# Cross-attention in fp32 on one core: three score banks, values of two tiles per block, row sums in a maximum buffer

## The reference

```
xn     = layernorm(x) * gamma + beta            # x [2, 512, 1024]
Q      = split_heads(xn @ Wq.T)                 # 32 heads of 32
K = V  = split_heads(ctx)                       # ctx [2, 1024, 1024]
scores = einsum('bhsd,bhtd->bhst', Q, K) / sqrt(32)
scores = where(mask, scores, -inf)
attn   = softmax(scores, -1) @ V
out    = x + attn.reshape(2, 512, 1024) @ Wout.T
```

## Time and profile before

| | us |
|---|---|
| three runs | 741.23 median, 739.92 to 744.85 |
| the profiled execution | 742.85 |
| its span, first to last instruction | 741.0 |

### The profile page before, as it was taken

How to read it: one execution, slowest core, us unless ns; L and a number is a source line. 1 busy time by engine, 2 the same in 40 slices (tenths; PEclk the granted TensorE clock), 3 DMA queues, 4 the chain that set the end, 5 groups by cost and what they waited for, 6 DMA issues and landing times.

```text
span 741.0 us, 10854 instructions
## 1 busy us (share of the span) xinstructions
PE 692.4 (93%) x3585; PEld 397.8 (54%) x3585; DVE 484.0 (65%) x496; ACT 350.1 (47%) x613; POOL 391.7 (53%) x106
## 2 busy tenths in 40 slices
PE   2789999878999999999999999999999999699998
PEld 2578788533444454444444444444444444378886
DVE  6762442057687878878788788887888677723231
ACT  3741112334565666656666566665665666300000
POOL 1000000047396797877978779688796798800000
PEclk9999999879999999999999999999999999999999
DMA  9620100515516235253351532515425104031331
GB/s 345 169 71 29 58 0 1 128 39 128 124 42 151 64 96 129 59 128 72 85 142 43 128 82 77 152 33 127 101 58 128 57 1 144 29 113 64 107 113 57
DMA packets 39518, 68.10 MB, mean 92 GB/s; under 512 B 5284, under 2 KB 21798, under 8 KB 39470
## 3 DMA queue, kind: packets, MB, share of 16 engines
q1 hardware_dynamic: 39444, 67.64, 33.2%
q10 hardware_dynamic: 36, 0.01, 0.0%
HBM read 25.18 MB, written 4.19 MB: 40 GB/s over the span
## 4 chain that ended last, share of the span: by engine, by line
PE 84%; DVE 6%; SPq 3%; DMA 2%; ACT 2%; issue 1%; POOL 1%; ACTq 0%; POOLq 0%; DVEq 0%
PE SX L903 18%; PE MX L883 17%; PE PV L919 16%; PE MX L1047 12%; PE SM L909 6%; PE PV L846 5%; PE SM L846 4%; DVE mx L703 2%; PE MX L823 2%; POOL acc L470 1%; PE MX L895 1%; PE SX L838 1%; DMA PR<-in_x 1%; PE MX L889 1%; ACT PR L504 1%
## 5 line engine op out<-in xcount | busy, mean ns | idle before, releaser
L703 DVE TENSOR_REDUCE mx<-MX 128x1 f32<-128x1024 f32 x256 | 303.1, 1220 | 139.6 <-PE MX L883 139.3
L587 ACT ACTIVATE PR<-SX 128x512 f32<-128x512 f32 x512 | 277.4, 594 | 187.4 <-PE SX L903 187.3
L470 POOL TENSOR_TENSOR acc<-acc,PR 128x2048 f32<-128x2048 f32 x64 | 293.5, 4586 | 31.9 <-ACT PR L587 25.4
L470 POOL TENSOR_TENSOR acc<-PR 128x2048 f32<-128x2048 f32 x16 | 73.3, 4580 | 222.0 <-ACT PR L587 143.5
L903 PE MATMUL SX<-R 99*128 99x512 f32 x512 | 180.1, 431 | 2.3 <-ACT PR L587 1.5
L883 PE MATMUL MX<-R 97*128 97x512 f32 x512 | 164.0, 417 | 17.0 <-DVE mx L703 7.2
L903 PEld LDWEIGHTS SX<-R 99*128 99x128 f32 x512 | 88.4, 189 | 112.2 <-ACT PR L587 91.8
L883 PEld LDWEIGHTS MX<-R 97*128 97x128 f32 x512 | 89.2, 189 | 105.1 <-DVE mx L703 63.3
L919 PE MATMUL PV<-PR,C 128*32 128x512 f32 x1024 | 138.7, 614 | 0.1
L1047 PE MATMUL MX<-R 128*128 128x512 f32 x192 | 46.8, 404 | 5.6 <-DVE R L782 5.6
L791 DVE TENSOR_TENSOR PR<-PR,MX 128x512 f32<-128x512 f32 x16 | 11.0, 688 | 58.5 <-PE MX L1047 56.9
(11 more groups left out here) (75 smaller groups left out, 517.7 us busy)
## 6 DMA issues: line engine op xcount, KB each, us to landing
R<-KTh SPq DMA_DIRECT2D x64, 256.0 KB, 4.3
PR<-in_x SPq DMA_DIRECT2D x16, 512.0 KB, 4.2
C<-in_ctx SPq DMA_DIRECT2D x16, 512.0 KB, 3.5
R<-KTl SPq DMA_DIRECT2D x64, 128.0 KB, 3.8
R<-QT SPq DMA_DIRECT2D x64, 128.0 KB, 2.5
acc<-in_L_xattn_Wq SPq DMA_DIRECT2D x8, 512.0 KB, 3.6
R<-QT SPq DMA_DIRECT2D x64, 64.0 KB, 2.1
C<-in_L_xattn_Wout SPq DMA_DIRECT2D x8, 512.0 KB, 3.2
```

The source lines that it names most:

```text
L470: nc.gpsimd.tensor_tensor(acc[:, :, :], a, PR[:, tt % RING, :, :], ALU.add).then_inc(pool_used, 1)
L587: nc.scalar.activation(PR[:, tt % RING, h, :], SX[h % 2][:, :], ACT.Exp, scale=SCALE).then_inc(exp_done, 1)
L703: nc.vector.tensor_reduce(mx[:, u % 2, c:c + 1], MX[par][:, :], mybir.AxisListType.X, ALU.max, negate=True).then_inc(mx_freed, 1)
```

## The change

- **Banks.** SM is gone; SX has three banks, used in turn. A score waits for the exp of the score three before it.
- **Slots.** A step is four slots of two tiles instead of eight tiles. A slot on TensorE: scores of heads 0, 1, 2 of the first tile; items; head 3; items; heads 0 and 1 of the second tile; items; heads 2 and 3; items; then values of the tiles `2k-1` and `2k` in one block.
- **Sums.** GpSimd adds tiles 0 to 5; tiles 6 and 7 and `acc` are multiplied by ones in one block, as an item `sums` in an MX buffer, at the end of slot 0 of the next step, right behind values of tile 7. `invert_sums` part 0 reads that buffer and frees it; parts 1 and 2 are in slot 1. So a step has 19 items, not 18. In the last step sums go to SX[0].
- **Bias.** The maxima lie as 16 columns in the order of the items, one transpose instead of four, and high and low parts are 16 x 128, not 4 x 512.
- **Queries.** `split_queries` stands after the first `max` of slot 0, not before `key_low`. SP issues the key rows before it waits for the split queries, and both before the load of values.
- **Items.** STEP and FIRST_STEP are new tables.

```diff
-POOL_TILES = (0, 1, 2, 4, 5, 6)
+BANKS = 3
+PROBS = TT * HPG
+POOL_TILES = (0, 1, 2, 3, 4, 5)
+DIRECT_TILES = (6, 7)
+GROUPED = [((0, 0), (0, 1), (0, 2)), ((0, 3),), ((1, 0), (1, 1)), ((1, 2), (1, 3))]
-SUMS_AT = (2, 5, 7)
+SUMS_AT = ((1, 0), (1, 1))
 FIRST_STEP = [
-    ([], []),
-    ([], maxima(1, 0, 1)),
...
+    ([], maxima(1, 0), maxima(1, 1), maxima(1, 2)),
...
 STEP = [
-    ([], keys(2)),
-    (maxima(1, 4), maxima(1, 5, 6)),
-    ([], maxima(1, 7, 8)),
-    ([], maxima(1, 9, 10)),
-    (maxima(1, 11), maxima(1, 12, 13)),
-    ([], maxima(1, 14, 15)),
-    ([], maxima(2, 0) + bias(1)),
-    (maxima(2, 1), maxima(2, 2, 3)),
+    (keys(2), maxima(1, 5), maxima(1, 6), maxima(1, 7) + sums(-1)),
+    (maxima(1, 8), maxima(1, 9), maxima(1, 10), maxima(1, 11)),
+    (maxima(1, 12), maxima(1, 13), maxima(1, 14), maxima(1, 15)),
+    (bias(1) + maxima(2, 0), maxima(2, 1), maxima(2, 2), maxima(2, 3, 4)),
 ]
...
             def bias_item(n, u, par):
-                for st in range(ST):
-                    ins = nc.tensor.transpose(MX[par][:, st * P:(st + 1) * P], mx[:, u % 2, st * HPG:st * HPG + P], ident[:, :])
-                ins.then_inc(bt_ready, 1)
+                nc.tensor.transpose(MX[par][:, 0:P], mx[:, u % 2, :], ident[:, :]).then_inc(bt_ready, 1)
...
+            def row_sums(n, bank):
+
+                for tt in DIRECT_TILES:
+                    sum_probs(bank, lambda h: PR[:, tt % RING, h, :], tt == DIRECT_TILES[0], False).then_inc(tile_used, 1)
                 pe.wait_ge(pool_used, ADDS * n + 2 * ADDS)
-                sum_probs(lambda h: acc[:, h, :], False, True).then_inc(sums_done, 1)
+                sum_probs(bank, lambda h: acc[:, h, :], False, True).then_inc(sums_done, 1)
...
+                for k, slot in enumerate(items):
+                    for j, (group, part) in enumerate(zip(GROUPED, slot)):
+                        for b, h in group:
+                            score(n, u, 2 * k + b, h)
+                        if j == len(slot) - 1 and k == 0 and not first:
+                            for item in part[:-1]:
+                                mx_item(*item)
+                            values(n - 1, u + RING - 1, TT - 1)
+                            mx_item(*part[-1])
                         else:
+                            for item in part:
+                                mx_item(*item)
+                    if k > 0:
+                        values(n, u, 2 * k - 1)
+                    values(n, u, 2 * k)
...
                 for k, slot in enumerate(items):
                     for j, part in enumerate(slot):
...
+                            if kind == "sums":
+                                invert_sums(n + a, 0, MX[at % 2][:, 0:S])
+                                dve.wait_ge(sums_turned, n + a + 1)
+                                dve.sem_inc(mx_freed, 1)
+                            at += 1
+                        if (k, j) == (1 if first else 0, 1) and n + 2 < STEPS:
+                            split_queries(n + 2)
```

More of the change, by code:

```diff
@@ L602, in high_and_bias, with step @@
                 return at
[L604 to L607, removed]
+            def step(n, items, at, first=False):
+                for k, slot in enumerate(items):
+                    for group, part in zip(GROUPED, slot):
+                        for b, h in group:
+                            exp(n, 2 * k + b, h)
+                        at = high_and_bias(n, part, at)
+                    if k == 0 and not first:
                         pv_copy(n - 1)
[L609 to L613, removed]
+            step(0, FIRST_STEP, FIRST_PARITY, first=True)
             with act.Fori(0, LOOPS) as j:
                 for u in range(1, RING + 1):
[L616 to L618 removed]
+                    step(RING * j + u, STEP, step_parity(u))
+            for n in APART[:-1]:
+                step(n, items_of(n), step_parity(n))
+            step(STEPS - 1, items_of(STEPS - 1), LAST_PARITY)
             pv_copy(STEPS - 1)
@@ L749, in wout_parts, with step @@
                                         ALU.subtract).then_inc(mx_freed, 1)
[L751 to L766, removed]
+            def step(n, u, items, at, first=False):
+                for k, slot in enumerate(items):
+                    for j, part in enumerate(slot):
+                        for kind, a, i in part:
+                            if kind == "keys":
+                                key_low(n + a, at % 2)
+                            if kind == "bias":
+                                bias_low(n + a, at % 2)
+                            if kind == "wout":
+                                wout_parts(i, at % 2)
+                            if kind == "max":
+                                maximum(n + a, u + a, i, at % 2)
+                            if kind == "sums":
[5 more added lines that the diff above has]
+                            split_queries(n + 2)
+                        if (k, j) in SUMS_AT and not first:
+                            invert_sums(n - 1, 1 + SUMS_AT.index((k, j)))
             step(0, 0, FIRST_STEP, FIRST_PARITY, first=True)
@@ new lines, in mx_item @@
+                def mx_item(kind, a, i):
+                    nonlocal at, freed, last_kind
+                    pe.wait_ge(mx_freed, freed - (kind != "bias" or last_kind != ("max", M_ITEMS - 1)))
+                    if kind == "keys":
+                        keys_item(n + a, u + a, at % 2, loads)
+                    elif kind == "bias":
+                        bias_item(n + a, u + a, at % 2)
+                    elif kind == "wout":
+                        wout_item(i, at % 2)
+                    elif kind == "sums":
+                        row_sums(n + a, MX[at % 2][:, 0:S])
+                    else:
+                        if first and i == 0:
+                            pe.wait_ge(rows_in[a], LATER_ROWS)
+                        max_item(n + a, u + a, i, at % 2)
+                    at += 1
+                    freed = freed + 1
+                    last_kind = (kind, i)
```

170 lines of the change are left out of this document (60 added, 110 removed).

## The result

The changed kernel takes **799.73 us** (median of 4 runs, 798.91 to 800.74), the kernel before on the same chip 743.04 (739.92 to 745.46): 1.0761 times as long, 95% interval 1.0732 to 1.0789. The forecast was 788, its range 764 to 812. The profiled execution took 800.44 us and its span is 798.6, 57.6 more than the span before.

What follows compares the result with a forecast made beforehand. TensorE was taken to bound the kernel, busy 692.4 of 741.0 us. Terms 38 (steps) + 4.5 (step 0) + 1.8 (end) + 2 (clock) = 46.3 on the profiled 742.85 gave 789, or 788 on the median's scale; range 764 to 812.

Steps and rivals of the forecast that it cites:

- The step: Steps 1 to 13: 33.5 us each with waits for MX, 2.9 more than before, 38 us in all; chance 0.62.
- The wait for keys: Slot 0: TensorE waits 1.6 us before maximum 6, until the buffer of keys comes back.
- the one before sums: End of slot 0: TensorE waits 0.7 us before sums, until maximum 6 frees its buffer.
- Slot 3: Last slot of a step: a wait of 1.25 us behind bias, then five maxima; 8.9 us instead of 6.3.
- The split: Query split on VectorE in slot 0: 1.1 us for both parts, with GpSimd idle, instead of 3.1.
- Rival 2: Slot 0: a GpSimd add catches the split, wait 2.7 us, 35.5 a step, 815 us; both slower rivals together 0.19.
- The clock: A few half-rate stretches in slots 0 and 3, at most 1.7 us each, 2 us in all.
- rival 1: Clock falls in each step, one stretch at 1.1 to 1.5 us, 803 to 808 us; both slower rivals together 0.19.
- Step 0: First step: 4.5 us more, bounds 0 and 8, from work moved behind the DMA wait and waits in later slots.
- the end: After step 15: two direct sums and acc stand together, 1.8 us more.
- Steps 14 and 15: Last two steps: wout items spread as before, change 0, bounds -1 and +2 us.
- What would show it: Signs: steps of 33 to 34 us, two waits in slot 0, four in slot 3, TensorE's share about 82%.

Runs made afterwards that it cites:

- experiment 1: Changed kernel with only the keys item of STEP moved behind maximum 7, before values of tile 7 and the sums; 777.27 us.
- experiment 2: Changed kernel with values of odd tiles moved behind the slot's second group of scores and its items, apart from the even tiles' values; 779.32 us.
- experiment 7: Changed kernel with only step 0's first slot reordered, all eight scores before the wait for the DMA; 798.57 us.
- experiment 9: The kernel of experiment 8 with the changed kernel's FIRST_STEP put back, one item fewer at its end; 737.84 us.
- experiment 8: The best version: changed kernel with keys late, odd-tile values behind the first score group, split_queries ahead of key_low, new item tables including step 0; 727.05 us.
- experiment 6: Kernel before the change with only each of its three sums blocks set right behind the values of its tile; 750.95 us.

## Why the prediction was right, and where it was not

**The step** held: 33.5 us forecast, 33.27 measured at full clock. Slot 0: 11.5 against 11.56. The wait for keys was 1.38 for 1.6, and the one before sums 0.47, with 0.19 before maximum 7, for 0.7. Slots 1 and 2 of step 9: 6.51 and 6.40 (482.38, 488.89, 495.29 are their first scores) for 6.7 and 6.4. Slot 3: 8.84 for 8.9, although its first wait was 0.88 for 1.25, because there the chain of five maxima sets the end, not the first wait. Experiments 1 and 2 show both ingredients: 1.9 us hang on where keys stands, 0.9 on the blocks in pairs, each in the slots where the edit is.

**The split** took 0.42 + 0.69 = 1.11 us in the steady steps, as forecast: GpSimd was idle beside it (0.00 busy in 475.60:479.00). Rival 2 did not come about in any of them. In step 0 the cast did meet an add:

```profile
161.98 4.55 POOL L475 TENSOR_TENSOR acc<-acc,PR 128x2048 f32<-128x2048 f32 x1 [1.04 <-ACT PR L592]
165.01 1.80 DVE L698 CAST QT<-QA 128x512 fp32r<-128x512 f32 x1
```

It ended at 166.81, 0.28 after the add, and the maximum behind it made TensorE wait 1.5 us. With the rule of the Trainium skill, SBUF — State Buffer, section "Who interferes with whom", these two rows agree as those before did.

**The clock** was mis-sized: the term was 2 us, and steps 1 to 13 alone lost 12.0, and step 0 more besides. It is a milder rival 1. Steps 7 to 13 each have one stretch, as that rival said, but it costs 0.86 us there (34.13 - 33.27), not 1.1 to 1.5, since the slower work covers the 0.47 of waiting before sums; while steps 3, 5 and 6 have none and steps 1 and 4 have 6.8 us or more. I had read from the page's line of the clock before that waits bring none; but the longest wait of a maximum for its buffer was 0.6 us there. The Trainium skill, TensorE: Matmul & The Clock Gate, section "A second HAM failure mode: psum-queue depth-cycling", describes just such a swing behind short idles; the trace agrees in steps 7 to 13 and not in step 6, where the same wait left the clock at 1.00.

**Step 0** was mis-sized too: 4.5 taken, 8 the upper bound, 10.0 measured. The step that failed is "its later slots have the waits above, where some stood before too". Of the 10.0 us, 6.0 are waiting: before, TensorE stood idle 10.5 + 1.5 us in step 0; after, 16.0 + 1.8 + 0.2 (the DMA's 10.5 instead of 5.8; behind keys 1.9 for 0.7; the bias item itself 1.8, where the item behind it waited 0.6; maxima 3.5 for 2.2; and 2.4 of waits for a query DMA, for exps and for the bias DMA are gone). The other 4.0 are work that takes longer: 30.7 us of step 0 lie at half rate, before 13.7. The first maximum starts 12.4 us after the first score now (151.85) and 12.3 before, so the whole loss stands behind it; by pairs of tiles step 0 took 14.2, 9.6, 10.0 and 12.9 us before and 18.8, 15.2, 9.5 and 13.2 now. That four scores came behind the DMA wait does not explain it (experiment 7). Where the items stand does, by experiment 9. Whether it is keys, which the best version puts ahead of the DMA wait, the spread over slots 1 to 3, or the cast that meets an add (1.80 us in the change, 2.60 in experiment 9, 0.42 in experiment 8) stays open.

**The rest**: the end +1.8, as forecast. Steps 14 and 15 -0.8, within the bounds. The sum: too little by 5.5 in step 0 and by 10 in the clock, too much by 3 in the steps (38 for 35), and 0.8 and 0.5 in the other places: 46.3 becomes 57.6. That the total is off by 11 and not by 15 is luck, since the errors of both signs take each other back in part; the length of a step is not, for its slots came out one by one.

**What would show it**: steps, runs and the two kinds of waits came as said (in slot 3 three waits show instead of four, in slot 0 three instead of two). TensorE's share did not: 88%, not 82%. The record has a reason. In slot 1 of step 9 the timeline shows no idle time, yet the slot takes 6.51 instead of 5.76: maximum 10 starts at 485.13, 0.52 us behind the score before it instead of 0.23, just when the maximum in its buffer is reduced (483.86 + 1.22). Such waits of 0.1 to 0.3 us show as longer matmuls and wider distances between starts, and work at half rate counts as busy. VectorE's 56% instead of 61% are the split that became cheap (19.4 + 22.6 us before) and `bias_low` (10.8, now 4.5).

## What to carry to other kernels

Joining small blocks saves on TensorE what the two prices of a block say, and takes from the engine behind it the time in which it would have been fed. In experiment 6, with two buffers between them, the second was the larger: 0.9 us a step saved by the prices, and 1.3 lost, since the step grew by 0.4. Between an item with a long way back (three engines, 3.5 us) and the next user of its buffer there must stand as much other work: lay out the order by these distances first, then join what is left. A wait that is short in itself can cost more on top through the clock, so take the waits away one and all: two edits gave 22.5 and 20.4 us apart, and 51.4 together.

## What the runs showed of the hardware that was not expected

- The same wait of 1.4 us behind 1.9 to 2.0 us of work brought a half-rate stretch in steps 7 to 13 and none in steps 3, 5 and 6; in experiment 1 a wait of 0.89 us (2.32 us of 3.40 busy) brought one of 6.8 us. Filling the waits with matmuls whose results nobody uses took the stretches behind them away, and 7 us off the time, at no cost in the length of steps 1 to 13.
- A stretch of 3.4 us at half rate cost 0.86 us of the step in the changed kernel and 0.7 to 1.3 in experiment 2, one of 6.8 us 2.2 to 2.5.
- With four scores more ahead of the long DMA wait of step 0 the low clock there lasted 3.4 us longer (17.1 for 13.7, one profile each), and the time was 798.57 for 799.73.
- `bias_high` and `bias_low` on 16x128 instead of 4x512 took 0.25 and 0.28 us instead of 0.59 and 0.68: a quarter of the columns made them shorter although four times the partitions took part.
- The cast of 128x512 took 0.42 us beside an idle GpSimd. Each of the 34 casts in these profiles that took longer (1.0 to 2.6 us) ended 0.28 or 0.29 us behind the end of a GpSimd add.
